# One transformer layer on one core: latents' root in three parts, head 0's maxima ahead of rotation products, next input loaded in heads 2 and 3

## The reference

```python
x = x + attn(layernorm(x))
x = x + ffn(layernorm(x))
# attn
q = rmsnorm(h @ wq_a.T, q_norm_w) @ wq_b.T          # latents 384, heads 16 x (128 + 64)
kv = h @ wkv_a.T                                     # 128 + 64
kv_c = rmsnorm(kv[..., :128], kv_norm_w)
k_pe = rope(kv[..., 128:]); q_pe = rope(q_pe)
out = softmax(q . k * scale) @ v;  out @ wo.T
# ffn
y = (silu(x @ q8(gate_w) * gs) * (x @ q8(up_w) * us)) @ q8(down_w) * ds
```

## Time and profile before

| | |
|---|---|
| median of 3 runs | 2305.53 us (2305.02 to 2308.83) |
| the profiled execution | 2308.34 us, its span 2306.0 us |
| TensorE busy | 2222.7 us, 96% |
| VectorE, ScalarE, GpSimd busy | 1590.2, 1062.1, 956.2 us |
| mean granted TensorE clock | 0.994 |

### The profile page before, as it was taken

How to read it: one execution, slowest core, us unless ns; L and a number is a source line. 1 busy time by engine, 2 the same in 40 slices (tenths; PEclk the granted TensorE clock), 3 DMA queues, 4 the chain that set the end, 5 groups by cost and what they waited for, 6 DMA issues and landing times.

```text
span 2306.0 us, 36511 instructions
## 1 busy us (share of the span) xinstructions
PE 2222.7 (96%) x10952; PEld 1027.7 (45%) x10952; DVE 1590.2 (69%) x3334; ACT 1062.1 (46%) x2335; POOL 956.2 (41%) x657
## 2 busy tenths in 40 slices
PE   6899989999999999999999999999999999999988
PEld 5334444445444454444544445444454445444443
DVE  7688877877558774677647776477655877567762
ACT  4466564444344543445425453354533454345532
POOL 1336335363344523455334543446324363343322
PEclk9999999999999999999999999999999999999999
DMA  6265633554144531545206451164513554144420
GB/s 249 64 147 131 128 85 85 121 111 97 24 116 105 121 66 28 138 103 121 56 20 153 103 119 46 38 146 103 116 28 79 121 112 96 23 99 107 102 62 18
DMA packets 698513, 218.37 MB, mean 95 GB/s; under 512 B 680208, under 2 KB 680464, under 8 KB 697360
## 3 DMA queue, kind: packets, MB, share of 16 engines
q1 hardware_dynamic: 698384, 216.77, 41.2%
HBM read 40.78 MB, written 8.39 MB: 21 GB/s over the span
## 4 chain that ended last, share of the span: by engine, by line
PE 73%; DVE 14%; ACT 4%; issue 4%; DMA 2%; SPq 2%; POOL 0%; DVEq 0%; ACTq 0%; POOLq 0%
PE bank L762 11%; PE bank L272 8%; PE bank L274 8%; PE bank L273 8%; PE scores L772 6%; PE bank L621 4%; PE bank L623 4%; PE bank L622 4%; PE scores L610 4%; PE scores L274 4%; PE scores L273 4%; PE scores L272 4%; DVE arena L1254 3%; DMA arena<-arena 2%; PE scores L607 2%
## 5 line engine op out<-in xcount | busy, mean ns | idle before, releaser
L1436 POOL TENSOR_TENSOR arena<-arena 128x1024 f16<-128x1024 f32 x256 | 545.0, 2129 | 709.3 <-ACT arena L926 709.3
L924 ACT ACTIVATE arena<-scores,shift 128x512 f32<-128x512 f32 x512 | 357.3, 698 | 600.4 <-DVE shift L1234 589.0
L1254 DVE SCALAR_TENSOR_TENSOR arena<-bank,rden,arena 128x512 f32<-128x512 f32 x512 | 350.7, 744 | 149.5 <-PE bank L274 149.5
L1232 DVE TENSOR_REDUCE mx<-scores 128x1 f32<-128x512 f32 x512 | 353.0, 689 | 10.1 <-PE scores L274 4.9
L926 ACT ACTIVATE arena<-scores,shift 128x512 f16<-128x512 f32 x512 | 358.5, 700 | 0.0
L762 PE MATMUL bank<-arena,WFF 128*128 128x512 f16 x1408 | 319.5, 381 | 12.9 <-DVE arena L1319 11.0
L1474 POOL TENSOR_TENSOR arena<-arena 128x512 f16<-128x512 f32 x96 | 114.8, 1196 | 323.3 <-ACT arena L980 323.3
L1038 DVE SCALAR_TENSOR_TENSOR arena<-bank,arena 128x512 f16<-128x512 f32 (+2 forms) x269 | 179.6, 669 | 58.6 <-ACT arena L917 53.9
L762 PEld LDWEIGHTS bank<-arena,WFF 128*128 128x128 f16 x1408 | 137.5, 98 | 181.2 <-DVE arena L1319 14.8
L272 PE MATMUL bank<-WVO,arena 128*128 (+1 forms) x512 | 194.1, 379 | 10.1 <-DVE arena L1038 10.1
L610 PE MATMUL scores<-arena 128*128 128x512 f16 x512 | 195.4, 382 | 0.0
(11 more groups left out here) (164 smaller groups left out, 3477.5 us busy)
## 6 DMA issues: line engine op xcount, KB each, us to landing
arena<-arena SPq DMA_TRANSPOSE x706, 2.7
arena<-w_ffn SPq DMA_DIRECT2D x24, 384.0 KB, 3.4
arena<-x SPq DMA_DIRECT2D x8, 1024.0 KB, 5.4
out<-arena SPq DMA_DIRECT2D x32, 256.0 KB, 2.3
arena<-x SPq DMA_DIRECT2D x14, 512.0 KB, 3.9
WFF<-w_o SPq DMA_DIRECT2D x4, 1024.0 KB, 18.6
arena<-w_nope SPq DMA_DIRECT2D x4, 768.0 KB, 14.0
arena<-down_scale SPq DMA_DIRECT2D x8, 256.0 KB, 3.3
```

What stands on the lines that cost most here:

```text
L924: act.activation(P32[:, t, :], SC[:, t, :], ACT.Exp, scale=EXP_SCALE, bias=shift[:, t:t + 1], accum_out=esum[:, par, t:t + 1]).then_inc(s[ ...
L1232: dve.tensor_reduce(mx[:, t:t + 1], SC[:, t, :], AX_X, ALU.max).then_inc(s["mxr"], 1)
L1254: dve.scalar_tensor_tensor(out=XR[:, t, :], in0=OBANK[t][:, :], scalar=rden[:, t:t + 1], in1=XR[:, t, :], op0=ALU.mult, op1=ALU.add).then_ ...
L1436: pool.tensor_tensor(PL[:, par, two, :], P32[:, two, :], PH[:, par, two, :], ALU.subtract).then_inc(s["pl"], 1)
```

## The change

Left out of the diff below: two hunks that replace the semaphore `ld_x` by one for each half of the input.

- In the FFN, `latents_norm` is made in three parts (4, 4 and 5 operations), after the products of chunks 0, 1 and 2, where all 13 stood after chunk 0's. The queries are split by ScalarE in chunks 2 and 3 (before 1 and 2) and by VectorE in 3 and 4 (before 2 and 3), the keys in 4 and 5 (before 3 and 4).
- At the start of attention VectorE takes head 0's maxima before the products of rotation group 5, and the products of group 7 move behind head 1's maxima. GpSimd makes its half of head 0 before it rotates group 5.
- The next input is loaded by halves in heads 2 and 3, each between the high and the low transposes, where both loads stood after head 1.

```diff
@@ -358,13 +359,15 @@
                 sp.dma_start_transpose(PT[:, par, 1, two].rearrange("p t k q -> p (t k) q"),
                                        PL[:, par, two, :].rearrange("p t k -> p (t k)")).then_inc(p_t[par][half], 16)
 
-            def head(i, base, par, ahead=True):
+            def head(i, base, par, ahead=True, between=None):
                 g = base + i
                 if ahead:
                     sp.wait_ge(s["sp"], NT * g + NT)
                     rope_rows(i + 2, par)
                     prob_rows_hi(g, par, 0)
                     prob_rows_hi(g, par, 1)
+                    if between:
+                        between()
                     prob_rows_lo(g, par, 0)
                     prob_rows_lo(g, par, 1)
                 else:
@@ -379,15 +382,14 @@
                 sp.wait_ge(s["f_b"], c - 1)
                 sp.dma_start(f_ring[f_set(c)], w_ffn[:, c * FC:(c + 1) * FC]).then_inc(f_ld[c % 2], 16)
 
-            def next_input(b):
-
+            def next_input(b, half):
+
+                two = slice(2 * half, 2 * half + 2)
                 sp.wait_ge(s["qkv"], (b + 1) * 2 * NT)
                 if isinstance(b, int) and b == 0:
                     sp.wait_ge(s["qpel"], N_ROT)
-                for half in range(2):
-                    two = slice(2 * half, 2 * half + 2)
-                    sp.dma_start(XN[:, two], xb[bass.ds(b + 1, 1), :, two].rearrange("a p t d -> (a p) t d")).then_inc(
-                        s["ld_x"], 16)
+                sp.dma_start(XN[:, two], xb[bass.ds(b + 1, 1), :, two].rearrange("a p t d -> (a p) t d")).then_inc(
+                    ld_x[half], 16)
 
             def turn_input(b, p, stg):
 
@@ -425,14 +427,15 @@
                 for i in range(NH):
                     if i == 6:
                         sp.wait_ge(s["qpel"], (b + 1) * N_ROT)
+                    between = None
                     if i == 1:
                         sp.wait_ge(s["rot"], (b + 1) * 2 * N_ROT)
-                    head(i, base, i % 2, ahead=i < NH - 2)
+                    if i in (2, 3) and not last:
+                        between = lambda: next_input(b, i - 2)
+                    head(i, base, i % 2, ahead=i < NH - 2, between=between)
                     if i == 0 and not first:
                         sp.wait_ge(s["stored"], b * (16 * NT))
                         sp.dma_start(XR, xb[bass.ds(b, 1)].rearrange("a p t d -> (a p) t d")).then_inc(s["ld_res"], 16)
-                    if i == 1 and not last:
-                        next_input(b)
                     if i in (11, 12) and not last:
                         turn_input(b, i - 11, stg)
                     if first:
@@ -989,10 +992,10 @@
                     if not last:
                         if c == 0:
                             kpe_hi(b + 1)
-                        if c in (1, 2):
-                            queries_hi(b + 1, 2 * c - 2)
-                            queries_hi(b + 1, 2 * c - 1)
-                        if c == 3:
+                        if c in (2, 3):
+                            queries_hi(b + 1, 2 * c - 4)
+                            queries_hi(b + 1, 2 * c - 3)
+                        if c == 4:
                             kv_hi(b + 1)
                     if first and NC_HEADS + c < NC_FF:
                         round_chunk(NC_HEADS + c)
@@ -1065,19 +1068,25 @@
                 w = WFF[:, c * FC:(c + 1) * FC]
                 dve.tensor_tensor(w, w, f_clip, ALU.add).then_inc(s["f_free"], 1)
 
-            def rsqrt(ch, v, n, eps):
+            def rsqrt(ch, v, n, eps, ops=range(RSQRT_OPS)):
 
                 ve, y, t = rs_v[:, 0:n], rs_y[:, 0:n], rs_t[:, 0:n]
-                if len(v.shape) == 3:
-                    ve, y, t = (q.rearrange("p (a b) -> p a b", a=v.shape[1]) for q in (ve, y, t))
-                ch.link(dve.tensor_scalar(ve, v, eps, None, ALU.add))
-                ve, y, t = rs_v[:, 0:n], rs_y[:, 0:n], rs_t[:, 0:n]
-                ch.link(dve.tensor_scalar(t.bitcast(I32), ve.bitcast(I32), 1, None, ALU.logical_shift_right))
-                ch.link(dve.tensor_scalar(y.bitcast(I32), t.bitcast(I32), -1.0, float(RSQRT_MAGIC), ALU.mult, ALU.add))
-                for _ in range(3):
-                    ch.link(dve.tensor_tensor(t, y, y, ALU.mult))
-                    ch.link(dve.scalar_tensor_tensor(out=t, in0=t, scalar=-0.5, in1=ve, op0=ALU.mult, op1=ALU.mult))
-                    ch.link(dve.scalar_tensor_tensor(out=y, in0=t, scalar=1.5, in1=y, op0=ALU.add, op1=ALU.mult))
+                for k in ops:
+                    if k == 0 and len(v.shape) == 3:
+                        ch.link(dve.tensor_scalar(ve.rearrange("p (a b) -> p a b", a=v.shape[1]), v, eps, None, ALU.add))
+                    elif k == 0:
+                        ch.link(dve.tensor_scalar(ve, v, eps, None, ALU.add))
+                    elif k == 1:
+                        ch.link(dve.tensor_scalar(t.bitcast(I32), ve.bitcast(I32), 1, None, ALU.logical_shift_right))
+                    elif k == 2:
+                        ch.link(dve.tensor_scalar(y.bitcast(I32), t.bitcast(I32), -1.0, float(RSQRT_MAGIC), ALU.mult,
+                                                  ALU.add))
+                    elif k % 3 == 0:
+                        ch.link(dve.tensor_tensor(t, y, y, ALU.mult))
+                    elif k % 3 == 1:
+                        ch.link(dve.scalar_tensor_tensor(out=t, in0=t, scalar=-0.5, in1=ve, op0=ALU.mult, op1=ALU.mult))
+                    else:
+                        ch.link(dve.scalar_tensor_tensor(out=y, in0=t, scalar=1.5, in1=y, op0=ALU.add, op1=ALU.mult))
 
             LN_N = 9 + RSQRT_OPS
             assert LN_N == 21
@@ -1122,7 +1131,7 @@
                     ch.link(dve.scalar_tensor_tensor(out=y, in0=t, scalar=1.5, in1=y, op0=ALU.add, op1=ALU.mult))
 
                 if part < 2:
-                    dve.wait_ge(s["ld_x"], b * 32 + 32)
+                    dve.wait_ge(ld_x[part], b * 16 + 16)
                     for k in (2 * part, 2 * part + 1):
                         ch.add(dve.bn_stats(bn[:, k, :], XN[:, k, :]))
                     ch.wait()
@@ -1142,14 +1151,18 @@
                     ch.link(dve.tensor_scalar(rs_x[:], y, XS, None, ALU.mult))
                 assert done + ch.n == (2, 4, 9, 15, 22)[part]
 
-            def latents_norm(a):
-                dve.wait_ge(s["ssq"], (a + 1) * 2 * NT)
-                ch = Chain(dve, "rms_chain", a * RMS_N)
-                rsqrt(ch, ss[:, :, :], 2 * NT, EPS_RMS)
-                ch.link(dve.tensor_scalar(rs_s[:, :, :], rs_y[:, :].rearrange("p (t c) -> p t c", c=2), QS * PROJ, None,
-                                          ALU.mult))
-                assert ch.n == RMS_N
-                dve.wait_ge(s["lat"], (a + 1) * 2 * NT)
+            def latents_norm(a, part=None):
+
+                first, end = (0, RSQRT_OPS) if part is None else ((0, 4), (4, 8), (8, RSQRT_OPS))[part]
+                if first == 0:
+                    dve.wait_ge(s["ssq"], (a + 1) * 2 * NT)
+                ch = Chain(dve, "rms_chain", a * RMS_N + first)
+                rsqrt(ch, ss[:, :, :], 2 * NT, EPS_RMS, range(first, end))
+                if end == RSQRT_OPS:
+                    ch.link(dve.tensor_scalar(rs_s[:, :, :], rs_y[:, :].rearrange("p (t c) -> p t c", c=2), QS * PROJ,
+                                              None, ALU.mult))
+                    assert first + ch.n == RMS_N
+                    dve.wait_ge(s["lat"], (a + 1) * 2 * NT)
 
             def keys_norm():
 
@@ -1259,6 +1272,8 @@
                 for c in chunks:
                     round_chunk(c)
                 maxima(g)
+                if i == 1:
+                    rot_products(b, N_ROT - 1, RBANK[(N_ROT - 1) % 2])
                 sums_of_head(g - 1, 1 - par)
                 if part in (0, 1, 2):
                     next_norm(b, part)
@@ -1276,12 +1291,11 @@
 
             def attention(b, last, first):
                 base = b * NH
+                maxima(base)
                 rot_products(b, N_ROT_FFN, RBANK[N_ROT_FFN % 2])
-                maxima(base)
                 qa_lo(base + 2, 0)
                 rot_products(b, N_ROT_FFN + 1, RBANK[(N_ROT_FFN + 1) % 2])
                 rot_lo(b, N_ROT_FFN)
-                rot_products(b, N_ROT_FFN + 2, RBANK[N_ROT_FFN % 2])
                 head_step(1, b, 1, chunks=chunks_of(1) if first else ())
                 for n in range(N_ROT_FFN + 1, N_ROT):
                     rot_lo(b, n)
@@ -1330,12 +1344,12 @@
                     if last:
                         continue
                     n = c - CHUNK_ROT
-                    if c == 0:
-                        latents_norm(b + 1)
-                    if c in (2, 3):
-                        queries_lo(b + 1, 2 * c - 4)
-                        queries_lo(b + 1, 2 * c - 3)
-                    if c == 4:
+                    if c < 3:
+                        latents_norm(b + 1, c)
+                    if c in (3, 4):
```

(9 more changed lines are left out.)

## The result

The changed kernel takes **2318.58 us** (median of 5 runs, 2316.78 to 2324.45) against 2305.53 (5 runs, 2304.60 to 2308.83): ratio 1.0057, 95% interval 1.0046 to 1.0069, slower. The forecast was 2311.3 in a range of 2296 to 2321. Sign and range are right; the time is 7.3 us over the forecast, and that has to be explained. One run of the kernel before, among the 14 taken beside e5, e6, e8 and e9, took 4717.03 us; it is left out of every median and ratio here. The profiled execution of the changed kernel took 2316.78 us, its span 2314.6: 8.6 us over the span before. It is the fastest of its five runs, and the one of before (2308.34) is 2.8 us over its median, so the traces show 8.6 of the 13 us between the medians. All lines after the change lie 1 to 14 further down (values L624, gate L765, chunk product L1333, maxima L1245, low transposes L359, next input L391).

A forecast was written before the change was run, and what follows sets the result against it. TensorE, busy 96% of the span, was taken as the bound, through its idle time and clock. FFN -9.1, attention +11.5 and clock +3.4 gave +5.8 us, 2311.3 us against the median of 2305.53; range 2296 to 2321.

The forecast's parts named there:

- FFN, -9.1: FFN: waits for VectorE shrink, gaining 6.4 us in batches 1 to 6 and 2.6 in batch 0.
- Head 0's maxima first: Start of attention, batches 2 to 6: first maximum 1.21 us earlier, so the wait at head 0's values goes.
- (b): TensorE's wait at head 0's values for the last transposed probabilities, 0.86 us in batch 2; forecast to move to the output projection.
- Head 1, 2.0 us: Head 1's values: new wait of 2.0 us for transposes held by GpSimd's late rotation of group 7.
- Attention without load and clock, +11.5: Attention, all batches: +5.2 us in batches 2 to 6, +1.8 in 1, +2.1 in 7, +2.4 in 0.
- The load, taken as 0: Half loads ahead of low transposes: head 2's landing just covered, cost 0, bounds 0 and +1 us for six batches.
- 3 us to spare: Head 3's low transposes behind the half load: 3 us of slack, so no wait there.
- unmoved: Head 2's chain starts at VectorE at its old time while TensorE comes 2.0 us later, covering the wait at its values.
- Rival (4): The load hits head 2's transposes, 1 us in six batches: 2317.3 us; chance 0.11.
- Clock, +3.4: Behind head 1's new holes: one low-clock stretch each in batches 1 and 7, +3.4 us, bounds 0 and +13.6.

The follow-up runs named there:

- e5: The changed kernel with both input loads back behind head 1 and group 7's products back ahead of head 1's maxima: 2296.73 us against 2306.41, ratio 0.9959.
- e6: e5, with GpSimd rotating group 5 between its two halves of head 0: 2291.81 us, ratio 0.9938 to the kernel before.
- e8: The kernel before with the next input's halves loaded in heads 2 and 3, each behind the low transposes: 2311.56 us, ratio 1.0025.
- e9: The kernel before with a 256-byte load between high and low transposes of heads 2 and 3, its tile ahead of the arena: 2312.41 us, ratio 1.0026.
- e1: The kernel before with the FFN part alone (root chain in three parts, splits one chunk later): 2298.49 us against 2306.35, ratio 0.9965.
- e4: The changed kernel with both input loads back behind head 1: 2308.07 us, ratio 1.0005 to the kernel before.
- e10: e9, with the small load's tile declared behind the arena instead of ahead of it: 2306.63 us, ratio 1.0000 to the kernel before.
- e7: e6, with VectorE's low parts of groups 6 and 7 behind head 2's step instead of head 1's, except in batch 0: 2294.81 us, ratio 0.9957.
- e3: The kernel before with only the next input's halves moved between high and low transposes of heads 2 and 3: 2331.75 us, ratio 1.0110.

## Why the prediction was right, and which step failed

- **FFN, -9.1.** Right: -8.8 in the trace, -9.2 when it stood alone. The holes of 1.07 us are gone in all six batches, no read of the latents came late, and batch 0's hole went from 5.58 to 3.44 against 3.5 forecast. Wrong in a detail: of the low clock in batch 0 nothing was given back in this execution. 16 matmuls took 6.41 us behind the shorter hole, 5.90 behind the longer, and batch 0 gained 1.62, not 2.6; in e1 they took 5.27, and it gained 2.26.
- **Head 0's maxima first; (b) only moves.** Right: the values of head 0 start 13.92 us after the first scores, not 14.95, and head 0's projection waits 0.46 to 1.15 us instead.
- **Head 1, 2.0 us.** Right in mechanism and size: 28.12 against 28.2 in the table, GpSimd's two rotations of group 7 took 0.84 us each as was taken, and the two runs e4 and e5 show that it hangs on the place of group 7's products.
- **Attention without load and clock, +11.5.** 9.3 alone: batches 2 to 6 lost 3.7, not 5.2. Head 1's values came 1.6 to 2.3 us later, 9.3 in these five and not 10.0; the other 0.8 was not placed. Batch 1's 2.1 (1.8 forecast), 7's 1.5 (2.1) and 0's 2.0 (2.4) are near.
- **The load, taken as 0: the step that failed.** It costs 10.5 us (changed kernel against e4), 1.7 of them the clock in batch 0. The forecast gave a half load half the delay of the 1 MB load, 0.7 us, to one transpose, and only at head 2; and it closed the matter for head 3 with "3 us to spare". Measured, both low transposes behind a half load land late, at head 3 the slower after 4.6 to 5.7 us instead of 2.8. For head 3 in batch 2: its last landing had 2.4 us to spare and TensorE is 1.3 later, 3.7 together; against it its transposes go out 2.6 later (2.0 because head 3's scores stand behind head 1's hole, 0.6 for the issue of the load) and land 1.7 later (0.85 of that also in e4, so not by the load). 3.7 - 4.3 = -0.6, and the wait is 0.61. The forecast asked only of head 2 whether its chain moves, and found it "unmoved"; that head 3's does move was left out. Rival (4), the load hits head 2's transposes, was the right kind at 0.11, with 6 us where there are 10.5.
- **Clock, +3.4.** Wrong in place. No hole of head 1 was followed by lower clock, in batches 1 and 7 neither. It fell in batch 0, behind the hole of 2.42 us ahead of head 2's values, where a half load stands too, as it fell behind the 2.16 us of the earlier trace rows. In the profiled executions the mean granted clock is 0.994 in both.
- **Time.** In the trace -8.8 + 20.3 - 2.35 - 0.5 = +8.6 against +5.8: load +10.5 unforeseen, the clock's 3.4 and 2.2 of attention not there, setup 2.35 faster by itself. These parts come from different executions and close to about half a us. In the medians +13: of the other 4.5 us, some 2.8 are the traced execution of before over its median and 1.8 that of the changed kernel under its own; they cannot be placed. That the time fell into the range is in part luck: 2311.3 + 10.5 = 2321.8 would have been outside, and the two terms taken too high made up for it.

## What to carry to other kernels

Before an operation is moved back on one engine, follow it to the queue that waits for its last reader: two products moved behind four maxima held SyncE's whole next head by a semaphore, and undoing that one move (e4 to e5) turned +1.7 us into -9.7. Price a transfer put ahead of small ones by the lateness of those behind it, for each head whose chain is itself already late, and never by its issue alone. And when an experiment adds a tile, look first at rows that it should not touch: a 16-byte tile slowed the median transpose by 0.5 us and nearly passed for the cost of a load.

## What was not expected of the hardware

- DMA transposes directly behind a 512 KB load on the same queue land late: the slower of the two after 4.6 to 5.7 us at head 3 of the changed kernel, 2.8 to 2.9 in batches 1 to 6 of the kernel before, 3.6 to 3.8 there in e4, which has the changed order without the load; behind a 256-byte load (e10) after 2.7 to 2.8 in five of seven batches and 3.6 in two. Head 2's are late without any load: 4.4 to 5.0 in the loop of the kernel before. The half loads themselves land after 4.3 us (median). The Trainium skill (DMA: Bandwidth & Descriptors, Queues, rings and completion order) says that each engine takes descriptors in ring order; the trace agrees as far as landings tell: in batch 2 the load issued at 705.26 landed at 709.15, the two transposes behind it at 711.07 and 711.86.
- The arena's place: 16 or 64 bytes further on, the median landing of a DMA transpose is 3.2 us instead of 2.7. Which places are fast was not tried beyond these two moves.
- The granted clock behind one long hole is not fixed. Batch 0's hole of 3.44 us was followed by 0.50 in the changed kernel, e1, e5 and e7, and by 1.00 in e4 and e6. Of e3's holes at head 2, those of 2.7 to 3.4 us in batches 1, 4, 5 and 6 were followed by 0.50, the one of 2.98 in batch 0 by 1.00. A hole of 2.03 us in batch 0 of e6 was followed by 0.50, one of 2.14 in batch 0 of e8 by 1.00. Behind the eight of 1.5 to 1.8 us at head 1 it stayed at 1.00. e6, then e3 in batch 0:

```profile
307.70:311.10 3.40, 3.40 (x16) 1.55 (x17) 3.19 (x9) 2.41 (x5) 1.16 (x1) 1.00 0.00 0
```

```profile
128.60:132.00 3.40, 3.38 (x16) 1.58 (x17) 1.58 (x3) 3.40 (x8) 3.01 (x2) 1.00 0.60 149
```
